# One core, hybrid attention/FFN block: four side steps of the second half placed later in TensorE's order

## The chip, the cores and the metric

The kernel runs on one core of one Trainium2 chip. The metric is the device time of one execution in microseconds (us). The kernel before takes 1200.9 us, the median of 3 runs (1200.29 to 1200.91). The five engines of the core are called PE (TensorE), DVE (VectorE), ACT (ScalarE), POOL (GpSimd) and SP (SyncE; here it only issues transfers). Each works through its own list of instructions in order and waits at semaphores that the others raise.

## The reference

```
x = L0_attn_a_x                                    # 16 batches x 512 tokens x 128 features, float32
x = x + attn_a(layernorm(x), w_qkv, w_out, b_out)  # 16 heads of 64, softmax of q over features, of k over tokens
x = x + ffn(layernorm(x), W_r, W_k, W_v, mu_r, mu_k)
x = x + attn_b(layernorm(x), W_Q, W_K, W_V, W_O)   # 16 heads of 8, rotary embedding, softmax(q k^T / sqrt(8)) v
x = x + ffn(layernorm(x), W_r, W_k, W_v, mu_r, mu_k)

def ffn(x):                                        # x_prev is x moved by one token
    xr, xk = mu_r*x + (1-mu_r)*x_prev, mu_k*x + (1-mu_k)*x_prev
    r = sigmoid(xr @ W_r.T);  k = xk @ W_k.T
    return r * (square(relu(k)) @ W_v.T)
```

## The kernel before, in words

The work is split into two halves. The first half runs attention A, the first FFN and the projections of attention B for all 16 batches, and keeps two results in DRAM. The second half, which the change touches, runs attention B and the second FFN. It is a pipeline over batches: iteration i computes the attention of batch i (the main work) and finishes batch j = i - 1 (the side work). There are 16 iterations with main work, 15 of these also with side work, and one last iteration with side work alone.

**The main work.** An iteration has 16 units, n = 0 to 15: four groups g of four heads, times four chunks of 128 keys. For each unit PE forms the scores of four heads (L1202) in two pairs. A pair is two matmuls into two banks of PSUM: heads 0 and 1 into banks 0 and 1, heads 2 and 3 into banks 2 and 3. ACT takes the exponential of each pair (L572, 128x1024). Then PE multiplies the exponentials with the values (`weigh_values`, L1221), one unit late: unit n's place in the order holds the weighing of unit n - 1. Before a pair of unit n, PE waits until ACT has read the same pair of unit n - 1, since the banks are the same.

```
if exists(s_exp.at(i, 2 * n + t - 1)):
    pe.wait_ge(s_exp.sem, s_exp.at(i, 2 * n + t - 1))
```

**The side work.** Behind the weighing of certain units PE does one side step, placed by an `if n == ...` written out by hand in `second_step`:

- n = 1 and 3: the transposes of the next batch's q and k (`kq_T`, L946, input `qk_rot`)
- n = 2: transposes of the second half of batch j's attention output (`u_transposes(j, 1, 6)`, L946, input `U`)
- n = 5: transposes of `c_tok`, which DVE copies out as `cT` (L887)
- n = 6: the output projection (L1265); DVE adds the residual (L865), takes the layer norm's statistics (L587 to L598), POOL forms the reciprocal root (L326), DVE normalises into `hn` (L605, four instructions)
- n = 9: the FFN transposes (`ffn_T`, L946, input `hn`), into bank 7; DVE mixes them with mu (L680, L686)
- n = 10: transposes of the first half of batch i's attention output (`u_transposes(i, 0, 6)`, L946, input `U`). They wait for DVE's copy of that half out of PSUM (`pv_copy(i, 0)`, L850)
- n = 12: the FFN projections for k and r (`ffn_kr`, L1050 and L1052), banks 6 and 7; ACT does relu and tanh (L470, L475) behind its exponentials of unit 12
- n = 14: the value projection (`ffn_v`, L1059), for which DVE squares (L694); DVE then gates and adds (L699, L702)

**What sets the order around them.** DVE's order in an iteration is: `pv_copy(j, 1)`, the splits of the next q and k, `normalise(j, 1)`, the copy to `cT`, `add_x3`, then

```
ln_norm(3, j, x1, hn)
...
pv_copy(i, 0)
...
mix(ffn[1], j, 7, True)
...
normalise(i, 0, 6)
...
square(ffn[1], j, 6)
...
gate_v(ffn[1], j, 6, x1, gated)
```

POOL's order is: `v_copy` (L400), `rope(i + 2)` (L384 to L386), the reciprocal root (L326), and right behind it `rope_sum(i + 2)` (L394), an addition of 128x1024.

SP's order in an iteration is: load x2 of batch i - 1 (L304), the stacks for g = 1 (eight transfers, L274, which fill `k_st` and `q_st` for units 4 to 7), the load of qkv (L263), the stacks for g = 2 and g = 3, the stacks for g = 0 of the next batch, then a wait for DVE's last FFN instruction (L702) and the store of the output of batch i - 1 (L314). The next iteration's list starts behind that store.

Of the kernel before, what the change touches and what calls it, by code (L numbers as in the profile page):

```python
# [30 lines left out]
def exists(value):  # L31

    return not isinstance(value, int) or value > 0
# [16 lines left out]
def hybrid_block(nc, x, w_qkv, w_out, b_out, W_Q, W_K, W_V, W_O, W_r, W_k, W_v, mu_r, mu_k,  # L50
# [22 lines left out]
    with ExitStack() as ctx:  # L73
# [106 lines left out]
        def there(batch):  # L180

            return not isinstance(batch, int) or 0 <= batch < NB
# [266 lines left out]
        def _(act):  # L449
# [18 lines left out]
            def relu(f, j, bank):  # L468
                act.wait_ge(f["k"].sem, f["k"].at(j))
                act.activation(k_relu[:, :], PS[:, bank, :], ACT.Relu).then_inc(f["relu"].sem, 1)  # L470

            def gates(f, j, bank):

                act.wait_ge(f["r"].sem, f["r"].at(j))
                act.activation(gate[:, :, :].rearrange("p c d -> p (c d)"), PS[:, bank, :], ACT.Tanh, scale=0.5)\  # L475
                   .then_inc(f["gate"].sem, 1)
# [88 lines left out]
            def second_half(i, p):  # L565
                for s in range(HB):
                    if there(i):
                        for t in range(2):
                            if t == 0 and exists(pv.at(i, s - NC + 1)):
                                act.wait_ge(pv.sem, pv.at(i, s - NC + 1))  # L570
                            act.wait_ge(s_mm.sem, s_mm.at(i, 2 * s + t + 1))
                            act.activation(probs[s % NC][:, 2 * t:2 * t + 2, :], PS[:, 2 * t:2 * t + 2, :],  # L572
                                           ACT.Exp).then_inc(s_exp.sem, 1)
                    if s == 12 and there(i - 1):
                        relu(ffn[1], i - 1, 6)
                        gates(ffn[1], i - 1, 7)

            over_batches(act, second_half, NB, 1, last=3)


# [336 lines left out]
        def _(pe):  # L917
# [250 lines left out]
            def maxima(i, g):  # L1168

                if exists(s_exp.at(i, 8 * g)):  # L1170
                    pe.wait_ge(s_exp.sem, s_exp.at(i, 8 * g))
                pe.wait_ge(k_in[g % 2].sem, k_in[g % 2].at(i, 64 * (g // 2) + 64))
                pe.wait_ge(q_in[g % 2].sem, q_in[g % 2].at(i, 64 * (g // 2) + 64))
                for m in range(8):
                    h, half = m // 2, m % 2
                    rows = slice(32 * h, 32 * h + 32)
                    if m >= 2:
                        pe.wait_ge(mx_ok.sem, mx_ok.at(i, 8 * g + m - 1))
                    for t in range(2):
                        c = 2 * half + t  # L1180
                        mm = pe.matmul(PS[:, c, :], q_st[g % 2][rows, c * P:(c + 1) * P], k_st[g % 2][rows, :],
                                       start=True, stop=True, tile_position=(32 * h, 0))
                    mm.then_inc(mx_mm.sem, 1)
                pe.wait_ge(mx_ok.sem, mx_ok.at(i, 8 * g + 8))
                for c in range(NC):
                    mm = pe.transpose(PS[:, 0, c * P:(c + 1) * P], row_max[:, c, :, :].rearrange("p h r -> p (h r)"),
                                      ident[:, :])
                mm.then_inc(mx_T.sem, 1)

            def scores(i, n, t, guarded):  # L1190

                g, kc = n // NC, n % NC
                if kc == 0 and t == 0:
                    pe.wait_ge(k_in[g % 2].sem, k_in[g % 2].at(i, 64 * (g // 2) + 64))
                    pe.wait_ge(q_in[g % 2].sem, q_in[g % 2].at(i, 64 * (g // 2) + 64))
                    if guarded:
                        pe.wait_ge(mx_neg.sem, mx_neg.at(i, g + 1))
                if exists(s_exp.at(i, 2 * n + t - 1)):
                    pe.wait_ge(s_exp.sem, s_exp.at(i, 2 * n + t - 1))
                for h in (2 * t, 2 * t + 1):  # L1200
                    rows = slice(32 * h, 32 * h + 32)
                    mm = pe.matmul(PS[:, h, :], k_st[g % 2][rows, kc * P:(kc + 1) * P], q_st[g % 2][rows, :],  # L1202
                                   start=True, stop=not guarded, tile_position=(32 * h, 0))
                    if guarded:
                        mm = pe.matmul(PS[:, h, :], ones_sq[rows, :], neg_c[rows, :], start=False, stop=True,
                                       tile_position=(32 * h, 0))
                mm.then_inc(s_mm.sem, 1)

            def weigh_values(i, n, p):

                g, kc = n // NC, n % NC
                u, e = g // 2, g % 2
                if n % 8 == 0:

                    if exists(pv_sb.at(i, u - 1)):
                        pe.wait_ge(pv_sb.sem, pv_sb.at(i, u - 1))
                    pe.wait_ge(v_ok.sem, v_ok.at(i))
                pe.wait_ge(s_exp.sem, s_exp.at(i, 2 * n + 2))
                for h in range(4):
                    at = 32 * (4 * g + h) - 16 * e  # L1220
                    mm = pe.matmul(PS[32 * h:32 * h + 32, 4 + u, :], v_flat[p][:, kc, at:at + 32],  # L1221
                                   probs[kc][:, h, :], start=(n % 8 == 0), stop=(n % 8 == 7),
                                   tile_position=(0, 32 * h), skip_group_check=True)
                mm.then_inc(pv.sem, 1)
# [5 lines left out]
            def second_step(i, p, guarded):  # L1230
                j = i - 1
                f = ffn[1]
                main, side = there(i), there(j)
                for n in range(HB):
                    if main:
                        if guarded and n % 4 == 0:
                            maxima(i, n // 4)
                        scores(i, n, 0, guarded)
                        scores(i, n, 1, guarded)
                    if main and n >= 1:  # L1240
                        weigh_values(i, n - 1, p)
                    if side and n == 0:
                        weigh_values(j, HB - 1, 1 - p)
                    if n == 1 and there(i + 1):
                        if exists(f["gate"].at(j - 1)):
                            pe.wait_ge(f["gate"].sem, f["gate"].at(j - 1))
                        kq_T(i + 1, 0, 7)
                    if n == 2 and side:
                        if exists(f["x"].at(j - 1, 1)):
                            pe.wait_ge(f["x"].sem, f["x"].at(j - 1, 1))  # L1250
                        u_transposes(j, 1, 6)
                    if n == 3 and there(i + 1):
                        pe.wait_ge(split.sem, split.at(i + 1, 2))
                        kq_T(i + 1, 1, 7)
                    if n == 5 and side:
                        if exists(f["gate"].at(j - 1)):
                            pe.wait_ge(f["gate"].sem, f["gate"].at(j - 1))
                        if there(i + 1):
                            pe.wait_ge(split.sem, split.at(i + 1))
                        pe.wait_ge(u_norm.sem, u_norm.at(j))  # L1260
                        four_transposes(lambda c: c_tok[:, c, :], 7).then_inc(ct_ps.sem, 1)
                    if n == 6 and side:
                        pe.wait_ge(ct_sb.sem, ct_sb.at(j))
                        for c in range(NC):
                            mm = pe.matmul(PS[:, 6, c * D:(c + 1) * D], cT[:, c * P:(c + 1) * P], WOT,  # L1265
                                           start=True, stop=True)
                        mm.then_inc(o_mm.sem, 1)
                    if n == 9 and side:
                        ffn_T(f, 3, j, 7)
                    if n == 10 and main:  # L1270
                        if exists(x3_ok.at(j)):
                            pe.wait_ge(x3_ok.sem, x3_ok.at(j))
                        u_transposes(i, 0, 6)
                    if n == 12 and side:
                        if main:
                            pe.wait_ge(u_norm.sem, u_norm.at(i, 2))
                        ffn_kr(f, j, 6, 7)
                    if n == 14 and side:
                        ffn_v(f, j, 6)

            pe.wait_ge(b_known.sem, b_known.at(0))
# [47 lines left out]
```

## Time and profile before

| | |
|---|---|
| median of 3 runs | 1200.9 us |
| the profiled execution: time, span | 1203.91 us, 1202.0 us |
| mean granted TensorE clock | 0.967 |
| busy in the span: PE, DVE, ACT, POOL | 1064.5, 691.8, 740.1, 428.4 us |
| DMA, mean over the span | 70 GB/s |
| exponentials of the second half (L572) | 512 instructions, 489.2 us busy, 103.9 us idle before them |
| first and last scores of the second half | 559.3 us and 1171.5 us |

The profile is of one execution, from the first to the last instruction (the span). Busy times are sums over one engine's instructions; matmuls are pipelined, so a busy PE is not PE at its peak. A row of the timeline has: start in us, time taken in us, engine, line, operation, output<-input with sizes, how many instructions are merged in the row, and in brackets how long the engine had been idle before it and what ended that idle time. "issue" there is a wait for nothing that the profile shows. PEld is PE's weight load, SPq the transfers that SP issues.

### The profile page before, as it was taken

The numbers are of one execution on the slowest core, as the hardware profiler recorded it, in microseconds if no ns is written. First come the engines' busy times: TensorE is split into PE (matmuls) and PEld (weight loads), VectorE is DVE, ScalarE is ACT, GpSimd is POOL, SyncE is SP. The second block draws the span as 40 slices with busy tenths as digits, with TensorE's granted clock in tenths as the row PEclk, the third lists the DMA queues.
The fourth block names the chain that finished last, engine by engine and source line by source line (L and its number), as shares of the span: only waits on it lengthen the run. The fifth ranks groups of instructions, "written<-read, shape, count | busy, mean of one in ns | idle before, by whom it ended". The sixth has DMA issues, their size and how long they took to land.

```text
span 1202.0 us, 20630 instructions
## 1 busy us (share of the span) xinstructions
PE 1064.5 (89%) x6999; PEld 649.0 (54%) x6999; DVE 691.8 (58%) x1652; ACT 740.1 (62%) x857; POOL 428.4 (36%) x339
## 2 busy tenths in 40 slices
PE   5999999999999999865999998999999998999993
PEld 4888888888888888752233333333333333333332
DVE  5688888888888888753145344433445344433333
ACT  3444444444444444313987888887888888888881
POOL 5545555555554555455123212331223212330000
PEclk9999999999999999965999999999999999999996
DMA  4011111111111111123323332333223332332211
GB/s 146 10 33 48 54 52 52 52 52 52 52 52 52 44 43 44 45 90 107 80 76 98 99 86 68 103 102 96 65 83 96 98 90 63 102 101 71 65 42 29
DMA packets 62246, 84.00 MB, mean 70 GB/s; under 512 B 10481, under 2 KB 36978, under 8 KB 62194
## 3 DMA queue, kind: packets, MB, share of 16 engines
q1 hardware_dynamic: 62194, 83.34, 23.0%
q8 instruction: 29, 0.48, 0.2%
q14 instruction: 23, 0.19, 0.1%
HBM read 28.77 MB, written 20.97 MB: 41 GB/s over the span
## 4 chain that ended last, share of the span: by engine, by line
PE 49%; DVE 19%; issue 15%; ACT 10%; POOL 2%; DMA 2%; SPq 2%; DVEq 0%; ACTq 0%; POOLq 0%
PE PS L1221 11%; ACT work L572 9%; PE PS L1202 9%; PE PS L1017 6%; PE PS L946 5%; PE PS L951 4%; DVE work L605 3%; PE PS L953 3%; PE PS L952 3%; PE PS L1050 3%; DVE q_sum L644 3%; DVE st L587 2%; PE PS L1059 2%; DVE qk_norm L723 2%; PE PS L1052 1%
## 5 line engine op out<-in xcount | busy, mean ns | idle before, releaser
L572 ACT ACTIVATE work<-PS 128x1024 f32<-128x1024 f32 x512 | 489.2, 1025 | 103.9 <-PE PS L1202 102.4
L1221 PE MATMUL PS<-work,v 128*32 128x512 f32 x2048 | 273.7, 607 | 1.1 <-ACT work L572 1.1
L1202 PE MATMUL PS<-q_st,k_st 32*128 32x512 f32 x1024 | 203.4, 498 | 40.3 <-ACT work L572 33.0
L1202 PEld LDWEIGHTS PS<-q_st,k_st 32*128 32x128 f32 x1024 | 80.1, 182 | 207.5 <-ACT work L572 167.9
L326 POOL TENSOR_TENSOR rs<-ve,half_neg 128x4 f32<-128x4 f32 x64 | 66.2, 1034 | 281.4 <-DVE ve L598 281.4
L462 ACT ACTIVATE work<-PS 128x1024 f32<-128x1024 f32 x64 | 65.7, 1026 | 155.7 <-PE PS L953 155.7
L337 POOL TENSOR_TENSOR work<-work,q_rcp 128x1024 f32<-128x1024 f32 x64 | 122.4, 1913 | 91.3 <-DVE q_rcp L648 91.3
L1017 PE MATMUL PS<-work 128*128 128x128 f32 x1024 | 128.3, 280 | 0.0
L1017 PEld LDWEIGHTS PS<-work 128*128 128x128 f32 x1024 | 124.5, 197 | 0.4
L400 POOL TENSOR_TENSOR v<-qkv_back,one 128x512 f32<-128x512 f32 x16 | 16.7, 1042 | 265.6 <-PE PS L1221 265.6
L951 PE MATMUL PS<-work_r,h1h 128*128 128x512 f32 x256 | 108.1, 422 | 1.7 <-DVE b_all L808 1.7
L953 PE MATMUL PS<-work_r,h1l 128*128 128x512 f32 x256 | 102.2, 399 | 0.0
L952 PE MATMUL PS<-work_r,h1h 128*128 128x512 f32 x256 | 101.8, 398 | 0.0
L466 ACT ACTIVATE work<-PS 128x1024 f32<-128x1024 f32 x64 | 65.6, 1025 | 40.8 <-PE PS L953 39.0
L644 DVE TENSOR_REDUCE q_sum<-work 128x16 f32<-128x1024 f32 x64 | 77.8, 1216 | 11.3 <-ACT work L462 7.0
L694 DVE TENSOR_TENSOR k_act<-PS,k_relu 128x512 f32<-128x512 f32 x32 | 22.1, 692 | 101.9 <-ACT k_relu L470 101.9
L605 DVE TENSOR_SCALAR hn<-x,mom,rs 128x128 f32<-128x128 f32 x128 | 62.6, 551 | 23.9 <-POOL rs L326 22.1
L1221 PEld LDWEIGHTS PS<-work,v 128*32 128x32 f32 x2048 | 40.4, 108 | 64.8 <-issue 61.6
L384 POOL TENSOR_TENSOR mask_cos<-qkv_back,cos_t 128x1024 f32<-128x1024 f32 x16 | 37.8, 2365 | 104.2 <-DMA qkv_back<-qkv_scratch 104.2
L699 DVE SCALAR_TENSOR_TENSOR gated<-gate,PS 128x512 f32<-128x512 f32 x32 | 22.0, 689 | 74.7 <-PE PS L1059 74.3
L946 PE MATMUL PS<-ident,work 128*128 128x128 f32 x128 | 21.2, 291 | 39.9 <-DVE work L605 39.9
L605 DVE TENSOR_SCALAR work<-x,mom,rs 128x128 f32<-128x128 f32 x64 | 54.2, 908 | 2.4 <-POOL rs L326 2.4
(144 smaller groups left out, 1596.7 us busy)
## 6 DMA issues: line engine op xcount, KB each, us to landing
qkv_scratch<-qkv_sb SPq DMA_DIRECT2D x16, 768.0 KB, 3.2
qkv_back<-qkv_scratch SPq DMA_DIRECT2D x16, 768.0 KB, 4.5
work<-in_attn_a_x SPq DMA_DIRECT2D x32, 256.0 KB, 3.0
x_scratch<-x SPq DMA_DIRECT2D x16, 256.0 KB, 2.1
k_st<-k_hi SPq DMA_DIRECT2D x64, 64.0 KB, 2.1
k_st<-k_lo SPq DMA_DIRECT2D x64, 64.0 KB, 2.1
q_st<-q_hi SPq DMA_DIRECT2D x64, 64.0 KB, 2.1
q_st<-q_lo SPq DMA_DIRECT2D x64, 64.0 KB, 2.1
```

What stands on the lines that cost most here:

```text
L326: pool.tensor_tensor(rs[:, :], ve[:, :], half_neg[:, :], ALU.pow).then_inc(rstd[n].sem, 1)
L337: pool.tensor_tensor(q3, q3, q_rcp[:, :].unsqueeze(2).to_broadcast([P, HA, DA]), ALU.mult)\
L572: act.activation(probs[s % NC][:, 2 * t:2 * t + 2, :], PS[:, 2 * t:2 * t + 2, :], ACT.Exp).then_inc(s_exp.sem, 1)
L605: dve.tensor_scalar(dst[:, c, :], src[:, c, :], mom[:, 0, c:c + 1], rs[:, c:c + 1], ALU.subtract, ALU.mult).then_inc(ln[n].sem, 1)
L644: dve.reduce_sum(q_sum[:, :], EQ[c].rearrange("p (h d) -> p h d", h=HA), AX_X).then_inc(q_rc.sem, 1)
L946: mm = pe.transpose(PS[:, bank, c * P:(c + 1) * P], src(c), ident[:, :])
L951: pe.matmul(dst, w[0], h[0], start=True, stop=False)
L952: pe.matmul(dst, w[0], h[1], start=False, stop=False)
L953: return pe.matmul(dst, w[1], h[0], start=False, stop=stop)
L1017: mm = pe.matmul(PS[:, 5 + a // 4, (a % 4) * P:(a % 4) * P + P], EK[c][:, cols], EQ[c][:, cols], start=(c == 0 and a % 4 == 0), stop=(c == ...
L1202: mm = pe.matmul(PS[:, h, :], k_st[g % 2][rows, kc * P:(kc + 1) * P], q_st[g % 2][rows, :], start=True, stop=not guarded, tile_position=(3 ...
L1221: mm = pe.matmul(PS[32 * h:32 * h + 32, 4 + u, :], v_flat[p][:, kc, at:at + 32], probs[kc][:, h, :], start=(n % 8 == 0), stop=(n % 8 == 7) ...
```

## The change

Five numbers change, four on PE and one on ACT. On PE the output projection goes from unit 6 to unit 7, the FFN transposes from 9 to 12, the projections for k and r from 12 to 14, and the value projection from 14 to 15. On ACT relu and tanh go from behind the exponentials of unit 12 to behind those of unit 14. The transposes of `U` at unit 10 and those at units 1, 2, 3 and 5 stay. DVE, POOL and SP keep their order. No instruction is added or removed.

```
                             act.activation(probs[s % NC]...
-                    if s == 12 and there(i - 1):
+                    if s == 14 and there(i - 1):
                         relu(ffn[1], i - 1, 6)
                         gates(ffn[1], i - 1, 7)
...
-                    if n == 6 and side:
+                    if n == 7 and side:
                         pe.wait_ge(ct_sb.sem, ct_sb.at(j))
...
-                    if n == 9 and side:
+                    if n == 12 and side:
                         ffn_T(f, 3, j, 7)
                     if n == 10 and main:
                         if exists(x3_ok.at(j)):
                             pe.wait_ge(x3_ok.sem, x3_ok.at(j))
                         u_transposes(i, 0, 6)
-                    if n == 12 and side:
+                    if n == 14 and side:
                         if main:
                             pe.wait_ge(u_norm.sem, u_norm.at(i, 2))
                         ffn_kr(f, j, 6, 7)
-                    if n == 14 and side:
+                    if n == 15 and side:
                         ffn_v(f, j, 6)
```

The first place is on PE, in an iteration of the second half, from the weighing of unit 7's place on. L1202 is the scores of one unit, L1221 a weighing, L946 with `hn` the FFN transposes, L946 with `U` the transposes of unit 10. Rows with a minus stand in the order before, rows with a plus in the changed one.

```order
 L1202 MATMUL PS<-q_st,k_st 128x512 x4
 L1221 MATMUL PS<-work,v_1 32x512 x4
+L946 MATMUL PS<-ident,U 128x128 x4
+L1202 MATMUL PS<-q_st,k_st 128x512 x4
+L1221 MATMUL PS<-work,v_1 32x512 x4
+L1202 MATMUL PS<-q_st,k_st 128x512 x4
+L1221 MATMUL PS<-work,v_1 32x512 x4
 L946 MATMUL PS<-ident,hn 128x128 x4
-L1202 MATMUL PS<-q_st,k_st 128x512 x4
-L1221 MATMUL PS<-work,v_1 32x512 x4
-L946 MATMUL PS<-ident,U 128x128 x4
```

The transposes of `U` stood one unit behind those of `hn`; now they stand two units ahead of them.

The second place is on PE too, at the end of the same iteration: L1059 is the value projection. The next iteration begins at the last unit of these rows.

```order
 L1202 MATMUL PS<-q_st,k_st 128x512 x4
 L1221 MATMUL PS<-work,v_1 32x512 x4
-L1202 MATMUL PS<-q_st,k_st 128x512 x4
-L1221 MATMUL PS<-work,v_1 32x512 x4
 L1059 MATMUL PS<-W7T,k_act 128x128 x4
 L1202 MATMUL PS<-q_st,k_st 128x512 x4
 L1221 MATMUL PS<-work,v_1 32x512 x4
 L1202 MATMUL PS<-q_st,k_st 128x512 x4
-L1221 MATMUL PS<-work,v_1 32x512 x4
-L1202 MATMUL PS<-q_st,k_st 128x512 x4
```

Between the projections for k and r, which stand ahead of these rows, and the value projection there are now the scores and the weighing of one unit, where there were two; and one unit less lies between the value projection and the next iteration.

## Rows read from the trace of the kernel before

**Rows 1.** Stretch, its us, busy PE, PEld, DVE, ACT, POOL, clock, DMA share, GB/s
```profile
700.00:800.00 100.00, 92.02 (x632) 34.43 (x624) 39.39 (x79) 82.52 (x90) 21.36 (x14) 1.00 0.33 95
```

**Rows 2.** Waits from 600 to 1140 us: who, for whom, us, times, longest
```profile
PEld PS L1202 <- ACT work L572: 144.3, 229, 1.1
ACT work L572 <- PE PS L1202: 81.9, 125, 1.7
PE PS L946 <- DVE hn L605: 14.9, 13, 1.2
```

**Rows 3.** Timeline of PE, units 4 to 10 of one iteration, unit 0 of the next
```profile
720.55 0.61 PE L1202 MATMUL PS<-q_st,k_st 32*128 32x512 f32 x4
...
722.17 0.49 PE L1202 MATMUL PS<-q_st,k_st 32*128 32x512 f32 x2
...
725.10 0.51 PE L1202 MATMUL PS<-q_st,k_st 32*128 32x512 f32 x4
...
726.54 1.16 PE L1265 MATMUL PS<-W7T,cT 128*128 128x128 f32 x8
...
727.62 0.51 PE L1202 MATMUL PS<-q_st,k_st 32*128 32x512 f32 x4
...
729.25 0.50 PE L1202 MATMUL PS<-q_st,k_st 32*128 32x512 f32 x2
...
731.59 0.91 PE L1202 MATMUL PS<-q_st,k_st 32*128 32x512 f32 x4
...
734.64 0.66 PE L946 MATMUL PS<-ident,hn 128*128 128x128 f32 x4 [1.16 <-DVE hn L605]
...
735.23 0.51 PE L1202 MATMUL PS<-q_st,k_st 32*128 32x512 f32 x4
...
749.87 0.50 PE L1202 MATMUL PS<-q_st,k_st 32*128 32x512 f32 x2
```

**Rows 4.** Timeline, units 12 to 15 of the iteration before, and unit 0
```profile
702.58 1.12 PE L1050 MATMUL PS<-mixed_k,W7T 128*128 128x512 f32 x2
...
703.74 0.60 ACT L470 ACTIVATE k_relu<-PS 128x512 f32<-128x512 f32 x1 [0.70 <-PE PS L1050]
704.37 0.69 DVE L694 TENSOR_TENSOR k_act<-PS,k_relu 128x512 f32<-128x512 f32 x1 [4.08 <-ACT k_relu L470]
...
704.52 0.51 PE L1202 MATMUL PS<-q_st,k_st 32*128 32x512 f32 x4
...
708.54 1.16 PE L1059 MATMUL PS<-W7T,k_act 128*128 128x128 f32 x8
...
709.63 0.50 PE L1202 MATMUL PS<-q_st,k_st 32*128 32x512 f32 x4
...
711.25 0.50 PE L1202 MATMUL PS<-q_st,k_st 32*128 32x512 f32 x2
```

**Rows 5.** Timeline of DVE and POOL, from the output projection on
```profile
727.80 0.69 DVE L865 TENSOR_TENSOR x<-PS,x 128x512 f32<-128x512 f32 x1 [1.90 <-PE PS L1265]
...
731.37 2.37 POOL L394 TENSOR_TENSOR qk_rot<-mask_cos,rot 128x1024 f32<-128x1024 f32 x1
731.50 3.08 DVE L605 TENSOR_SCALAR hn<-x,mom,rs 128x128 f32<-128x128 f32 x4 [1.21 <-POOL rs L326]
...
734.51 0.68 DVE L850 COPY U<-PS 128x512 f32<-128x512 f32 x1
...
738.49 0.42 DVE L858 TENSOR_TENSOR c_tok<-PS,den_rcp 128x256 f32<-128x256 f32 x1
```

**Rows 6.** Timeline of DVE: the same normalisation in iteration 14
```profile
1118.22 1.12 DVE L605 TENSOR_SCALAR hn<-x,mom,rs 128x128 f32<-128x128 f32 x4 [1.21 <-POOL rs L326]
```

**Rows 7.** Timeline of SP, from the store of an output on
```profile
711.28 0.42 SPq L314 DMA_DIRECT2D out<-gated  x1
...
716.75 1.23 SPq L274 DMA_DIRECT2D q_st<-q_lo  x2
```

**Rows 8.** DMA issues from 640 to 1100 us: KB each, median us to landing
```profile
q_st<-q_lo SPq DMA_DIRECT2D x48, 64.0 KB, 2.1
```

More of the change, by code:

```diff
@@ L573, in second_half @@
                                            ACT.Exp).then_inc(s_exp.sem, 1)
-                    if s == 12 and there(i - 1):
+                    if s == 14 and there(i - 1):
                         relu(ffn[1], i - 1, 6)
@@ L1261, in second_step @@
                         four_transposes(lambda c: c_tok[:, c, :], 7).then_inc(ct_ps.sem, 1)
-                    if n == 6 and side:
+                    if n == 7 and side:
                         pe.wait_ge(ct_sb.sem, ct_sb.at(j))
@@ L1267, in second_step @@
                         mm.then_inc(o_mm.sem, 1)
-                    if n == 9 and side:
+                    if n == 12 and side:
                         ffn_T(f, 3, j, 7)
@@ L1273, in second_step @@
                         u_transposes(i, 0, 6)
-                    if n == 12 and side:
+                    if n == 14 and side:
                         if main:
@@ L1277, in second_step @@
                         ffn_kr(f, j, 6, 7)
-                    if n == 14 and side:
+                    if n == 15 and side:
                         ffn_v(f, j, 6)
```

## The prediction

> **What bounds the kernel now.** I read the stretches of time first. In the second half PE is busy 92% and ACT 83% of the time, at the full granted clock of 1.00 [rows 1]: neither is full, so no sum of busy times gives the time. The view of waits says why. PE's scores wait for ACT's exponentials and ACT's exponentials wait for PE's scores [rows 2]: the two run as a chain through the four banks of the scores. So the place of a side step counts, and not its time alone. The third wait that is seen is of the FFN transposes for DVE's `hn`, 1.2 us in nearly every iteration [rows 2, 3]. The timeline of PE then gives the lengths of units, from one start of scores to the next. They fall into three kinds:
>
> - A late unit stands behind a side step: both pairs go at once, the weighing follows 0.44 us later and takes 1.0. With a side step s it is 1.44 + s long (unit 6: 725.10 to 727.62, 2.52, where s is the output projection, 1.08). Without one the next first pair must wait for an exponential, and it is 1.62 long (unit 4: 720.55 to 722.17; unit 7: 727.62 to 729.25) [rows 3].
> - A punctual unit stands behind a late one without a side step: its second pair waits for ACT. It is 2.34 + s long (unit 8: 729.25 to 731.59, 2.34; unit 5: 722.17 to 725.10, 2.93, which is 2.34 + 0.59 for four transposes) [rows 3].
> - A unit behind a punctual one without a side step has its pairs 0.41 us apart (unit 9's row takes 0.91 instead of 0.50), so it is 0.41 + 0.44 + 1.0 = 1.85 + s long [rows 3].
>
> The side steps take: transposes 0.59; output projection 1.09; value projection 1.09 (708.54 to 709.63); projections for k and r 1.94 (702.58 to 704.52) [rows 3, 4]. Starts of unit 4 and of the next unit 0 are 29.32 us apart (720.55, 749.87), and starts of unit 0 and unit 4 are 9.30 apart (711.25, 720.55): a period of 38.62 [rows 3, 4].
>
> **The change part by part.** The same instructions are issued, so all of it is waits and the kinds of units.
>
> *The FFN transposes at unit 12.* Their wait of 1.16 to 1.2 us goes: `hn` will be ready long before. What is late next stands behind `hn` in DVE's order: `pv_copy(i, 0)`, for which the transposes of `U` at unit 10 wait. Before, it was done (734.51 + 0.68 = 735.19) before PE wanted it.
>
> *The output projection at unit 7.* It starts the chain that ends in `hn` and in that copy. From its start to DVE's addition it is 1.26 us (726.54 to 727.80), to the end of `hn` 8.04 (731.50 + 3.08 = 734.58), to the end of the copy 8.65 [rows 3, 5]; PE follows 0.05 later, at 8.70. In the new order PE comes to the transposes of `U` 1.09 (the projection) + 1.62 (late unit 8) + 2.34 (punctual unit 9) + 1.85 (unit 10 up to its side step) = 6.90 us after the projection's start. So PE waits there 1.80 us, where it waited 1.2 before. Behind the waiting transposes are the scores of unit 11, and ACT runs dry. The wait has moved and grown. Its bounds are 0 (if `hn` took 1.12 us as it does where POOL has nothing beside it [rows 6], the chain would be 1.96 shorter) and 2.5 (if one more instruction of the chain were held by POOL for 0.7 us, about the length of one copy, since POOL's rotary products for the next batch start later too, behind the later store); I take 1.80, which the rows of the same chain give.
>
> *The units from 4 to 15 in the new order:* late 1.62; punctual with transposes 2.93; late 1.62; punctual with output projection 3.43; late 1.62; punctual 2.34; unit 10 with wait and transposes 1.85 + 1.80 + 0.59 = 4.24; late 1.62; punctual with FFN transposes 2.93; late 1.62; punctual with k and r 2.34 + 1.94 = 4.28; late unit 15 with the value projection 1.44 + 1.09 = 2.53. The sum is 30.78 against 29.32 now: +1.46 us, of which the wait is 0.6 and the rest comes from side steps that stood in neighbouring units (5 and 6, 9 and 10) and now stand alone, each behind a pair of a late and a punctual unit.
>
> *Units 0 to 3.* Now unit 15 is a late one without a side step (709.63 to 711.25) and unit 0 a punctual one. After, unit 0 is late (1.62), unit 1 punctual (2.93), unit 2 late (2.03); for unit 3, which follows a side step but finds ACT behind, I take 2.5. That is 9.1 instead of 9.30: -0.2.
>
> *Value projection, relu and tanh.* Relu starts 1.16 us after the k projection (702.58, 703.74) and the square ends 2.48 after it (704.37 + 0.69) [rows 4]. The value projection's turn comes 1.94 + 1.44 = 3.38 after it, so the missing unit is covered with 0.9 us to spare: no wait. If that cover failed it would be a wait of some tenths. FFN transposes to k and r: DVE's mixing and normalising lie between, from 734.64 to 738.49 + 0.42 = 738.91 [rows 3, 5], 4.27 us. The new turn is 0.59 + 1.62 + 2.34 = 4.55 later: no wait either, with some 0.2 to spare.
>
> *SP's queue.* The value projection now ends right ahead of unit 0. DVE gates and adds behind it, and the store of the output is issued 2.74 us after the projection's start (708.54, 711.28) [rows 4, 7]. With unit 0 starting 1.09 after the projection, the store is issued at 1.65 after unit 0's start; now it is at 0.03. Behind the store in SP's order are the load of x2 and the eight transfers that fill the inputs of units 4 to 7. The last of them is issued at 717.39 (the second of the two in 716.75 + 1.23) and lands 2.1 us later [rows 7, 8], at 719.5: 8.2 us after the store. Now unit 4 starts 9.30 after unit 0 and has 1.05 to spare. After, the data is there at 1.65 + 8.2 = 9.85 and unit 4's turn is at 9.1: a wait of 0.75 us. The trace shows no such wait, so its bounds are 0 (nothing, if SP's issues close up) and 1.65; I take 0.75.
>
> The Trainium skill bears on the first term (SBUF — State Buffer, "Who interferes with whom"): VectorE in its two-port mode and GpSimd exclude each other for whole instructions, and whoever starts first has the port. The rows agree: four instructions of DVE take 3.08 us beside POOL's `rope_sum` and 1.12 without it [rows 5, 6], and POOL had started first, 731.37 against 731.50. By that rule a reversed start would free DVE and remove the wait; since `rope_sum` stands right behind the reciprocal root in POOL's order, whenever the projection comes, I expect the same start and the 3.08 again.
>
> **The sum.** The period grows by 1.46 - 0.2 + 0.75 = 2.0 us in the twelve iterations 2 to 13: 24.1. Iteration 1 has no store ahead of it: 1.3. Iterations 14 and 15 have no `rope_sum`, so neither order waits for `hn`; the kinds of units and the store leave some 1.3 each: 2.6. The last iteration starts behind the later value projection: 0.5. Together +28.5 us. On the profiled execution's 1203.9 that is 1232.4; the median of the runs is 3.0 below that execution, so the forecast for the median is 1200.9 + 28.5 = 1229.4, rounded to 1229.
>
> **The rivals.**
> 1. *Only the transfers are in time* (the waits as above, but SP's late start is absorbed): 14 x 0.75 less, +18, 1219. For it: 1.05 us to spare now, which is a lot against 1.65. Against it: the eight issues are of fixed length.
> 2. *The wait goes and nothing takes its place*: faster. This needs DVE to start `hn` ahead of POOL's addition, so that the copy ends 1.96 us earlier and the transposes of `U` don't wait. Then units 4 to 15 take 30.78 - 1.80 = 28.98, 0.34 less than now, and with units 0 to 3 it is -0.54 in thirteen iterations: -7, 1194; with the wait for the transfers as well it is +0.2 each, +3, 1204. Against it: 0.13 us between the two starts, the same way round each time, since all such waits of the profile are of one length, 1.2 at most.
> 3. *The chain to the copy grows* by the 0.7 us of the upper bound: twelve times 0.7 more, +37, 1237. For it: the later store moves POOL's rotary products 1.6 us later. Against it: the output projection moves later as well, by some 2.4 us in its iteration, so the two don't come nearer.
> 4. *The change does nothing to the time*, if ACT set the period: ACT idles 18% [rows 1] and waits for PE 125 times [rows 2], so it does not.
>
> **How the numbers follow.** Forecast 0.72, rival 1 0.13, rival 2 0.06 (half of it faster, half near no change), rival 3 0.07, rival 4 0.02. The range reaches from rival 1 with a little off its side to just short of rival 3: 1217 to 1236. What a measurement can tell from no change here is about 0.2%, 2.4 us: faster 0.04, same 0.03, slower 0.93.
>
> **What would show it.** In the changed profile: the transposes of `hn` wait for nothing; the transposes of `U` at unit 10 wait about 1.8 us for DVE's copy L850; the scores of unit 4 wait about 0.75 us for a transfer into `q_st`; the store of the output comes 1.6 us behind unit 0's start; the period from unit 0 to unit 0 is 40.6 us in the middle. The prediction is wrong if `hn` takes 1.1 us in the middle iterations, if unit 10 does not wait, or if the period stays below 39.

## The result and the profile after

The changed kernel takes 1237.28 us, the median of 4 runs (1234.79 to 1241.12); the kernel before 1200.6 (4 runs). The ratio is 1.031, with a 95% interval of 1.028 to 1.034: slower by 37 us, where +28.5 was forecast and the range ended at 1236. The profiled execution has a span of 1235.4 us.

First the waits of PE and ACT in the middle of the second half of the changed kernel (who, for whom: us in total, times, longest):

```profile
PEld PS L1202 <- ACT work L572: 157.2, 221, 1.7
...
ACT work L572 <- PE PS L1202: 112.6, 117, 3.1
...
PE PS L946 <- DVE U L850: 23.0, 13, 1.8
```

The wait for `hn` of [rows 2] is gone. In its place PE waits 13 times for DVE's copy L850, 1.8 us at most, and ACT's waits for scores are longer, up to 3.1 us where they were 1.7.

The timeline around one such wait, the answer to [rows 3] and [rows 5]:

```profile
862.76 1.16 PE L1265 MATMUL PS<-W7T,cT 128*128 128x128 f32 x8
...
864.03 0.69 DVE L865 TENSOR_TENSOR x<-PS,x 128x512 f32<-128x512 f32 x1 [4.42 <-PE PS L1265]
...
867.60 2.37 POOL L394 TENSOR_TENSOR qk_rot<-mask_cos,rot 128x1024 f32<-128x1024 f32 x1
867.73 3.09 DVE L605 TENSOR_SCALAR hn<-x,mom,rs 128x128 f32<-128x128 f32 x4 [1.20 <-POOL rs L326]
...
870.74 0.68 DVE L850 COPY U<-PS 128x512 f32<-128x512 f32 x1
...
871.48 1.11 PE L946 MATMUL PS<-ident,U 128*128 128x128 f32 x4 [1.76 <-DVE U L850]
872.52 0.80 PE L1202 MATMUL PS<-q_st,k_st 32*128 32x512 f32 x4
873.25 1.74 PE L1221 MATMUL PS<-work,v 128*32 128x512 f32 x8
874.91 0.93 PE L1202 MATMUL PS<-q_st,k_st 32*128 32x512 f32 x4
875.77 1.06 PE L1221 MATMUL PS<-work,v 128*32 128x512 f32 x8
```

From the projection (862.76) to PE's transposes (871.48) it is 8.72 us; forecast 8.70, and a wait of 1.80. So far the rows are as forecast. What they show besides is that PE's own work behind the wait is slow: four transposes in 1.11 us instead of 0.66, a weighing in 1.74 instead of 1.06. The busy times and the clock of the same stretches (us; the columns are those of [rows 1]) point to the reason, which the fill run below tests:

```profile
868.00:870.00 2.00, 1.71 (x12) 0.34 (x10) 2.00 (x2) 1.81 (x3) 1.97 (x1) 1.00 0.00 0
870.00:872.00 2.00, 0.53 (x3) 0.53 (x4) 1.42 (x5) 0.29 (x1) 0.00 (x0) 0.81 0.00 0
872.00:874.00 2.00, 2.00 (x11) 0.68 (x13) 0.00 (x0) 0.65 (x1) 0.00 (x0) 0.50 0.00 0
874.00:876.00 2.00, 2.00 (x16) 0.53 (x12) 0.00 (x0) 1.83 (x3) 0.00 (x0) 0.84 0.32 81
```

PE was busy for 0.53 of 2 us, and the granted clock falls, to 0.81 on the mean of these 2 us and to 0.50 in the next: the lower of its two levels, 1.2 GHz instead of 2.4. In the second half before its last iteration the changed kernel has 12 such stretches, 48 us in all; the kernel before has none there. Ten of them begin in the last 0.2 us of the wait at unit 10 or up to 1.4 us behind it; three of the 13 waits there are followed by none. The other two begin 2.4 and 2.5 us behind a wait of unit 4's scores for a transfer, 1.19 us long (ending at 684.57) and 1.75 (at 728.81). The Trainium skill describes this gate (TensorE: Matmul & The Clock Gate, Part 1): the chip sets the matrix engine's clock, full or half, by how busy the engine has been. The trace agrees in that every one of the 12 falls comes at the end of a wait of 1.19 us or more or shortly behind it. Over a long stretch it is this row, against 1.00 in [rows 1]:

```profile
640.00:1100.00 460.00, 406.94 (x2686) 149.72 (x2688) 181.73 (x375) 349.70 (x378) 106.70 (x66) 0.95 0.29 83
```

SP's queue in the changed kernel, the answer to [rows 7], with the scores of unit 4:

```profile
1009.55 0.41 SPq L314 DMA_DIRECT2D out<-gated  x1
...
1014.79 1.23 SPq L274 DMA_DIRECT2D q_st<-h3l  x2
...
1017.80 0.61 PE L1202 MATMUL PS<-q_st,k_st 32*128 32x512 f32 x4 [0.75 <-DMA q_st<-h3l]
```

Unit 0 of this iteration starts at 1007.90, so the store is issued 1.65 us behind it, as forecast, and unit 4 waits 0.75 us for the last transfer (forecast 0.75). In every second iteration, where `q_hi` and `q_lo` are the source, the last transfer lands 7.5 us behind the store instead of 8.0 and PE waits about 0.2 us. The exceptions are the last wait of the trace for such a transfer (1.06 us) and the first two. In these two one issue into `k_st` takes 1.27 and 2.08 us instead of some 0.5, and PE waits 1.19 and 1.75 us:

```profile
684.57 0.61 PE L1202 MATMUL PS<-q_st,k_st 32*128 32x512 f32 x4 [1.19 <-DMA q_st<-h3l]
...
728.81 0.61 PE L1202 MATMUL PS<-q_st,k_st 32*128 32x512 f32 x4 [1.75 <-DMA q_st<-q_lo]
```

### The profile page after: what moved, and what is told of

The parts are those of the page before. It is cut to its first block, busy times and chain, and to the rows that moved or that the text cites. A ratio compares the mean times of both kernels' runs of the same rounds, so it can differ in the third digit from the quotient of the medians.

```text
span 1235.4 us, 20630 instructions
## 1 busy us (share of the span) xinstructions
PE 1075.6 (87%) x6999; PEld 647.4 (52%) x6999; DVE 692.9 (56%) x1652; ACT 737.9 (60%) x857; POOL 428.0 (35%) x339
## 4 chain that ended last, share of the span: by engine, by line
PE 46%; DVE 20%; issue 15%; ACT 9%; SPq 4%; DMA 3%; POOL 2%; DVEq 0%; ACTq 0%; POOLq 0%
PE PS L1221 10%; PE PS L1202 8%; ACT work L572 8%; PE PS L1017 6%; PE PS L946 5%; SPq L274 3%; DVE work L605 3%; PE PS L951 3%; PE PS L953 3%; PE PS L952 3%; PE PS L1050 3%; DVE q_sum L644 2%; DVE st L587 2%; DVE qk_norm L723 2%; PE PS L1059 1%
## 5 line engine op out<-in xcount | busy, mean ns | idle before, releaser
L1221 PE MATMUL PS<-work,v 128*32 128x512 f32 x2048 | 285.4, 631 | 0.0
L1202 PE MATMUL PS<-q_st,k_st 32*128 32x512 f32 x1024 | 201.6, 514 | 53.9 <-ACT work L572 38.3
L1202 PEld LDWEIGHTS PS<-q_st,k_st 32*128 32x128 f32 x1024 | 79.8, 189 | 229.7 <-ACT work L572 195.4
L1221 PEld LDWEIGHTS PS<-work,v 128*32 128x32 f32 x2048 | 41.0, 110 | 65.7 <-issue 62.8
L680 DVE TENSOR_SCALAR mixed_r<-PS,mu 128x512 f32<-128x512 f32 x16 | 12.0, 751 | 88.9 <-PE PS L946 88.9
L946 PE MATMUL PS<-ident,work 128*128 128x128 f32 x128 | 21.4, 292 | 41.0 <-DVE work L605 41.0
```

What stands on the lines that cost most here:

```text
L946: mm = pe.transpose(PS[:, bank, c * P:(c + 1) * P], src(c), ident[:, :])
```

## The experiments

Each was timed in three or more rounds against the kernel before on the same chip; the ratios are to that kernel, whose medians in these series were 1201.29, 1202.09 and 1202.86 us. Differences between medians of different series are therefore good to a microsecond or two. The comments in the lines of code below are for the reader and not in the kernels.

**The output projection back at unit 6.** All else as changed.

```
-                    if n == 7 and side:      # output projection
+                    if n == 6 and side:
```

> The changed kernel with the output projection back at unit 6; the other three steps stay late. Theory A (the cost hangs on the chain from the projection to DVE's copy, which the transposes of U wait for, and the half clock behind that wait): the chain starts about 2.4 us earlier, the wait of 1.76 us at unit 10 is gone or below 0.3, what is left is the wait for q_st at unit 4 (0.7 us in 14 iterations, some half clock behind it) against the gain of the FFN transposes' old wait; 1196 to 1204 us. Theory B (the late places as such cost, side steps no longer in neighbouring units): most of the loss stays, 1220 us or more.

Measured: 1198.61 us, ratio 0.997 (0.995 to 0.999). Theory A. Three of the four steps are late and the kernel is as fast as before or a little faster; in its profile no wait for L850 and no half clock is left ahead of the last iteration. One number of the five carries the whole loss: with it alone put back, the loss is gone.

**The output projection alone at unit 7.** All else as before.

> The kernel before with the output projection alone moved from unit 6 to 7. Theory A (the projection starts the chain that bounds the iteration): the FFN transposes at unit 9 now wait about 3 us for hn, PE stands still and the clock falls behind it: 1230 to 1245 us, as slow as the whole change or slower. Rival (the loss comes from the four steps together): 1201 to 1215.

Measured: 1265.46 us, ratio 1.052 (1.051 to 1.054). The mechanism was right and its size was not: the range of the expectation ended 20 us too low. The FFN transposes wait as expected, and the clock of the long stretch is the lowest of all runs:

```profile
PE PS L946 <- DVE hn L605: 35.5, 12, 3.0
```

```profile
640.00:1100.00 460.00, 395.73 (x2580) 146.04 (x2573) 179.03 (x370) 334.01 (x361) 105.56 (x66) 0.93 0.28 80
```

There are 13 stretches of half clock, one at each of the 13 waits, 72 us in all against 48 in the changed kernel. The waits themselves are 23.5 us longer than before (38.4 against 14.9 in 13 iterations); the other 40 us of the loss are the half clock and the lengths of the units, and no run separates these two here. With the projection at 7 the other moves together win 28 us back (26 by the ratios): PE meets DVE's chain one unit later, waits 1.76 us instead of 2.97 and has less half clock. That one of them costs by itself is shown by the value projection alone, below.

**Fill work at unit 10.** Twelve transposes of the identity matrix, whose result nothing reads, go in front of the transposes of `U`.

```
                         if exists(x3_ok.at(j)):
                             pe.wait_ge(x3_ok.sem, x3_ok.at(j))
+                        if side and not (isinstance(i, int) and i >= 14):
+                            for r in range(3):
+                                four_transposes(lambda c: ident[:, :], 7)
                         u_transposes(i, 0, 6)
```

> The changed kernel with twelve 128x128 transposes of the identity (about 1.75 us of PE work, output unused) in front of the transposes of U at unit 10, in iterations up to 13: PE is busy where it waited. Theory A (the granted clock falls to half for 3.4 us behind that wait, 11 times in the profile, at about 0.75 us each, and this is the 8 us by which the forecast fell short): the stretches of half clock behind unit 10 are gone, 1227 to 1231 us, close to the forecast of 1229. Rival (the missing 8 us are waits or unit lengths): 1236 to 1238 us, with or without the drops of the clock.

Measured: 1226.17 us, ratio 1.019 (1.018 to 1.021), a little below the expected range; 11 us less than the changed kernel by the medians, 14 by the ratios. The kernel does more work and is faster. Its timeline of PE:

```profile
983.15 1.53 PE L946 MATMUL PS<-ident 128*128 128x128 f32 x12
984.99 0.66 PE L946 MATMUL PS<-ident,U 128*128 128x128 f32 x4 [0.31 <-DVE U L850]
985.58 0.51 PE L1202 MATMUL PS<-q_st,k_st 32*128 32x512 f32 x4
986.01 1.06 PE L1221 MATMUL PS<-work,v 128*32 128x512 f32 x8
```

```profile
640.00:1100.00 460.00, 416.85 (x2900) 162.04 (x2900) 186.71 (x387) 358.92 (x388) 111.99 (x69) 1.00 0.31 86
```

The transposes of `U` still can't start before the copy, but the clock stays at 1.00 up to the last iteration and the transposes and the weighing have their old 0.66 and 1.06 us. The wait is only filled, and what follows it is faster: the half clock is a cost of its own. (The expectation counts 11 falls behind this wait; the trace has ten.) Not all of the gain need be the clock's, since PE also waits 2.4 us less for transfers than in the changed kernel (5.3 against 7.8 us in all), nearly all of it in the two iterations with the long waits shown above. An estimate for the clock alone is 9 to 11 us.

**Fill work at units 4 and 10.** Five more transposes of the identity in front of unit 4's scores.

```
+                        if n == 4 and side:
+                            pe.wait_ge(pv_sb.sem, pv_sb.at(i, 0))
+                            for r in range(5):
+                                pe.transpose(PS[:, 5, 0:P], ident[:, :], ident[:, :])
                         scores(i, n, 0, guarded)
```

> As the run with fill work at unit 10, and five more transposes of the identity (about 0.7 us) in front of the scores of unit 4, where they wait for q_st. Theory A: the clock stays full through the second half, 1224 to 1229 us. Rival (the wait at unit 4 does not move the clock): the same as the run with the fill at unit 10 alone, or up to 2 us more where the transfers are there before the fill ends.

Measured: 1229.07 us, ratio 1.021 (1.019 to 1.023): 3 us more than with the fill at unit 10 alone by the medians, 2 by the ratios, whose intervals overlap. The rival holds: nothing is gained. With unit 10 filled the clock was already full, so there was nothing to win at unit 4, and in every second iteration the fill (0.7 us) is longer than the wait.

**POOL's exchange, on the changed kernel and on the one before.** The addition `rope_sum` goes ahead of the reciprocal root.

```
-                if there(i - 1):
-                    rsqrt_var(3, i - 1)
                 if there(i + 2):
                     rope_sum(i + 2)
+                if there(i - 1):
+                    rsqrt_var(3, i - 1)
```

> The changed kernel with POOL's addition rope_sum ahead of the reciprocal root instead of behind it, so that it no longer runs beside DVE's four normalisations. Theory A: these take 1.1 us instead of 3.1, the copy of U's half is done in time, the wait of 1.76 us at unit 10 and the half clock behind it go; what is left is the wait for q_st at unit 4: 1237 - 12 x 1.8 - 11 = 1204 us, 1201 to 1208. Rival (the late places cost by themselves): above 1220.

> The kernel before with the same exchange on POOL. Theory A: hn is done 1.5 us earlier, the FFN transposes at unit 9 wait for nothing, the period falls from 38.6 to 37.6 in the twelve middle iterations: 1187 to 1190 us, faster than both kernels. Rival (the reciprocal root now waits for the rotary products, so the gain is lost): 1198 to 1203.

Measured: 1204.80 us on the changed kernel, ratio 1.002 (1.001 to 1.003); 1187.92 on the one before, ratio 0.988 (0.987 to 0.990). Both as theory A says. The changed kernel's timeline with the exchange:

```profile
844.28 2.37 POOL L394 TENSOR_TENSOR qk_rot<-mask_cos,rot 128x1024 f32<-128x1024 f32 x1
848.16 1.02 POOL L326 TENSOR_TENSOR rs<-ve,half_neg 128x4 f32<-128x4 f32 x1 [1.51 <-DVE ve L598]
849.28 1.12 DVE L605 TENSOR_SCALAR hn<-x,mom,rs 128x128 f32<-128x128 f32 x4 [1.20 <-POOL rs L326]
850.31 0.69 DVE L850 COPY U<-PS 128x512 f32<-128x512 f32 x1
```

The same four instructions of DVE take 1.12 us where they took 3.09. In the changed kernel the first of the four takes 2.32 us, until POOL's addition has ended, and the other three 0.33 each: DVE stood still while the addition ran. Taking that collision away makes the changed kernel 32 us faster, but the kernel before 14, so these 32 are not all the change's doing. With the exchange in both, the change still costs 17 us (1204.80 against 1187.92).

**The store later in SP's order, on the changed kernel.** The store of the output goes behind the eight transfers for units 4 to 7 and the load of qkv of the next iteration.

```
                     if g == 1 and there(i + 2):
                         load_back(i + 2)
+                    if g == 1:
+                        store_out(i - 2)
...
-                if there(i - 1):
-                    sp.wait_ge(ffn[1]["x"].sem, ffn[1]["x"].at(i - 1))
-                    sp.dma_start(out_view[i - 1], gated[:, :, :])...
+                if after_last(i):
+                    store_out(i - 1)
```

> The changed kernel with SP's store of the output moved behind the eight transfers for units 4 to 7 (and the load of qkv) of the next iteration. Theory A: the wait of the scores of unit 4 for q_st goes (0.75 us in 14 iterations, with the clock's drops behind it): 1223 to 1227 us; the wait at unit 10 and its half clock stay. Rival (another transfer or wait takes its place): 1235 to 1238.

Measured: 1228.49 us, ratio 1.022 (1.019 to 1.024), a little above the expected range. No wait of scores for a transfer is left, 9 us are won, and 9 stretches of half clock, 41 us, remain, all at the wait at unit 10.

**The value projection alone at unit 15.** All else as before.

> The kernel before with the value projection alone moved, from unit 14 to 15. Theory A (the store of the output is issued 1.6 us later and holds SP's transfers for units 4 to 7, as forecast with 0.75 us in 14 iterations): 1211 us, up to 1216 where the clock falls behind the wait; the scores of unit 4 wait for a transfer. Rival (the 1.05 us to spare absorb it): 1200 to 1203 us.

Measured: 1211.31 us, ratio 1.007 (1.005 to 1.009). Theory A: scores wait for `q_st`, which no row of the kernel before shows. The view of L1202 has (what PE idled for, us, times):

```profile
  DMA q_st<-h3l: 4.1, 5
  DMA q_st<-q_lo: 1.9, 5
```

**Both repairs, and fill with the later store.** The terms were then tested for adding up.

> The changed kernel with both repairs, POOL's exchange and SP's later store. Theory A (the two waits are separate and add): 1204.8 less the wait for q_st in 14 iterations, about 0.7 us each: 1193 to 1197 us, below the kernel before though all four steps stay late. Rival (the store's place gains nothing once unit 10 does not wait): 1202 to 1205.

> The changed kernel with the fill work at unit 10 and SP's later store: the full clock and no wait for q_st, with the wait for DVE's copy left (filled). Theory A (the terms add up): 1226.2 less 14 x 0.7 = 1216 us, 1214 to 1219; the remaining 15 us over the kernel before are the longer wait at unit 10 and the isolated side steps. Rival (the terms overlap): above 1221.

Measured: 1194.90 us, ratio 0.993 (0.992 to 0.995), for both repairs: 10 us below POOL's exchange alone. And 1218.69 us, ratio 1.013 (1.011 to 1.015), for fill and later store: 7.5 below the fill alone, at the upper end of what was expected. The terms add, within some 3 us. In the first of the two PE waits neither for `U` nor for a transfer in the middle iterations. The kernel before with the exchange on POOL has only two short waits left there, 0.8 and 0.5 us for `hn`, and the changed kernel is 7 us slower than that (1194.90 against 1187.92). This is about what the side steps in their late places cost by themselves.

**Better orders.** Two kernels on the base of the one before. The first has POOL's exchange and the projections for k and r at unit 13, relu and tanh behind unit 13. The second leaves POOL and SP as they were:

```
-                    if n == 9 and side:      # FFN transposes
+                    if n == 11 and side:
-                    if n == 10 and main:     # transposes of U, first half
+                    if n == 12 and main:
-                    if n == 12 and side:     # projections for k and r; relu and tanh also at 13
+                    if n == 13 and side:
```

> The kernel before with POOL's exchange (1187.9 us measured) and the projections for k and r at unit 13 instead of 12, relu and tanh behind unit 13: the side steps then stand in neighbouring units, 5 and 6, 9 and 10, 13 and 14. Theory A (a side step in the unit behind another one costs its own time alone, one that stands alone costs a late and a punctual unit around it): 0.7 us less in each of 15 iterations, 1176 to 1180 us. Rival (the place does not matter once nothing waits): 1186 to 1190.

> The kernel before without any change to POOL or SP: FFN transposes at unit 11, transposes of U at 12, projections for k and r at 13, value projection at 14, output projection at 6. Theory A: hn and the copy of U's half are done before PE comes to them, nothing waits, four side steps stand in four neighbouring units, and the store is issued as before: the period falls from 38.6 to about 36.9, 1176 to 1182 us. Rival (the mixing and normalising don't fit between units 11 and 13 and the projections wait): 1188 to 1200.

Measured: 1181.34 us, ratio 0.982 (0.980 to 0.984), and 1177.33 us, ratio 0.978 (0.976 to 0.980). Both beat the kernel before and the changed one. The second, in which four numbers change, is the fastest of all. In the first the move by one unit wins 6.6 us more than POOL's exchange alone (0.982 against 0.988), though it ends 1.3 above the expected range. Both kernels have at most two waits of 0.5 us or more for `hn`, none above 0.8, and in the middle iterations the period falls from 37.5 to 36.75 us: side steps in neighbouring units are cheaper than the same steps apart. In the kernel with unit 13 the clock is at half for 3.4 us in two late iterations (from 1077.21 and from 1124.99). The second of these comes 2.9 us behind a wait of 0.92 us for a transfer, the first behind idle times of 0.2 and 0.3 us only, so the length of one wait does not alone decide. The long stretch of the second:

```profile
640.00:1100.00 460.00, 438.96 (x3025) 166.32 (x3017) 204.21 (x430) 396.50 (x426) 117.44 (x73) 1.00 0.33 92
```

ACT is busy 86% there, against 83% before [rows 1] and 76% in the changed kernel.

## Why the prediction was wrong

Direction, places and waits were right. The time was outside the range by 1.3 us and 8 us above the forecast: one term of 9 us or more was missing, and a smaller error the other way hid part of it.

- *The step that failed* is the one on the clock: "at the full granted clock of 1.00", read from the kernel before, was carried over to a kernel in which PE waits longer. The forecast priced the wait at unit 10 as 1.80 us of standing still and nothing behind it. PE's clock then falls to half for 3.4 us or twice that in most iterations. The fill run prices it: 11 us by the medians, 14 by the ratios (1.0308 - 1.0194 = 0.0114, times 1200.6), of which some 2.4 can be shorter waits for transfers. It was not among the bounds, nor a rival. The kernel before has 13 waits of 1.1 to 1.2 us at the FFN transposes and no fall of the clock; the changed one has 13 of 1.76 at the transposes of `U` and 10 falls there; with the output projection alone at unit 7 there are 13 of 2.9 to 3.0 and 13 falls. With that step in the sum it would have been 39.5 to 42.5.
- *The wait that moves from the FFN transposes to the transposes of U* was right: 8.72 us of chain against 8.70, a wait of 1.76 against 1.80, and DVE's order as its cause, shown by the exchange on POOL and by the projection back at unit 6.
- *The kinds of units.* In the fill run, where the clock is full, transposes of `U` follow each other by 40.1 and 40.7 us in turn (944.88, 984.99, 1025.65), 1.8 more than 38.62 on the mean, where 2.0 was forecast. That neighbouring side steps are cheaper is shown by the run with unit 13. Apart from every wait their places cost 7 us (1194.90 against 1187.92); the sum has 1.46 - 0.6 - 0.2 = 0.66 for this in each of the twelve middle iterations, 8 us.
- *The store and the transfers* were right as a mechanism and in the iteration shown to 0.1 us. The term was 14 x 0.75 = 10.5; the runs give 10 (value projection alone), 9 (store later), 10 (store later with POOL's exchange) and 7.5 (with the fill). The size was taken from an iteration with one slow issue, in which the last transfer lands 8.2 us behind the store; later ones have 8.0 and 7.5 in turn. So the trace has a wait of about 0.75 in every second iteration, about 0.2 in the others, 1.19 and 1.75 in the first two and 1.06 in the last: 7.8 us over 11 waits, not 10.5 over 14.
- *The sum without the clock* was 28.5; the fill run has 1.0194 x 1200.6 - 1200.6 = 23.3. So the forecast was 5 us too high in the terms that it had and lacked 11 to 14 in the one that it hadn't. Had all been right but the clock, the miss would have been greater: that it was only 1.3 us outside the range is in part luck. Without its transfers the sum was 18.0; the fill run with the later store, which has neither half clock nor these waits, is 15.8 us above the kernel before (1218.69 against 1202.86), so the wait at unit 10 and the places were sized rightly within some 2 us.
- *The rival in which the transfers are in time* fell with the rows of unit 4. *The rival in which nothing takes the wait's place* fell for the changed kernel, and its mechanism was right: freed from POOL's addition, the changed kernel runs in 1204.80, where the rival, with the wait for the transfers left, said 1204; with the later store as well it runs in 1194.90, where the rival said 1194. *The rival of the longer chain* stands nearest to the measured 1237 in time only: its chain did not grow.
- *Value projection one unit behind k and r, and FFN transposes two units ahead of them*: no wait in the trace at full clock, as forecast.

## What to carry to other kernels

When a step is moved later, follow the chain that it starts, through the order of the engine that serves it, to the next thing that the busy engine asks of it: the visible wait goes, and one behind it in that order comes. A longer stall of TensorE can cost more than its length, by the slower clock behind it, so a forecast that lengthens a stall needs a bound for the clock, even if the trace of before shows a full one. To price a change, make the same repair on both kernels: a collision that both have is not the change's cost. A store that stands ahead of loads in one queue turns a late result into late inputs of the next iteration.

## What the runs showed of the hardware

PE's standing still for 1.76 us, in a loop in which it is busy 88% of the time, came with half clock for 3.4 us or twice that in 10 of 13 iterations; standing still for 2.9 to 3.0 us did so in 13 of 13. Waits of 1.1 to 1.2 us at the FFN transposes of the kernel before did so in none of 13, yet one wait of 1.19 us for a transfer in the changed kernel and one of 0.92 in the kernel with unit 13 were followed by half clock some 2.4 and 2.9 us later. Filling 1.53 us of the gap with useless transposes kept the clock at 1.00 up to the last iteration and made the kernel 11 us faster. And DVE's four normalisations of 128x128 took 3.09 us where POOL's addition of 128x1024 had started 0.13 us ahead of them and ran beside them, and 1.12 where it did not.
